# Attention output: query transposes two tiles ahead of the output products, output bias added by TensorE, norm statistics read from PSUM

## The reference

```python
q, k, v = split(x @ w_qkv)
q = softmax(q, axis=-1) / sqrt(64)
k = softmax(k, axis=1)
v = v / N
context = einsum('bnhd,bnhe->bhde', k, v)
out = einsum('bhde,bnhd->bhen', context, q) ... @ w_out + b_out
mu, var = mean(out, -1), mean((out - mu)**2, -1)
out = (out - mu) * rsqrt(var + 1e-5) * ln_scale
```

## Time and profile before

| | |
|---|---|
| Median of 3 runs | 2295.41 us (2293.19 to 2297.71) |
| The profiled execution | 2298.77 us, span 2297.0 us |
| Mean granted clock of PE | 0.968 |
| PE busy | 2076.6 us, 90% |
| DVE busy | 1340.3 us, 58% |
| ACT busy | 1045.3 us, 46% |
| Chain that ended last | PE 60%, DVE 14%, DMA 9%, issue 8% |

### The profile page before, as it was taken

One profiled execution on the slowest core, in us unless ns is written; L12 is line 12 of the kernel. 1 busy time (PEld: TensorE's weight loads), 2 busy tenths in 40 slices (PEclk: granted clock), 3 DMA queues, 4 the chain that ended last, 5 costly groups with the idle time before them and its releaser, 6 DMA issues.

```text
span 2297.0 us, 45572 instructions
## 1 busy us (share of the span) xinstructions
PE 2076.6 (90%) x13668; PEld 1497.5 (65%) x13669; DVE 1340.3 (58%) x2876; ACT 1045.3 (46%) x2324; POOL 628.5 (27%) x752
## 2 busy tenths in 40 slices
PE   4999788888888887899999999999599999879998
PEld 2544344344444445678888888888488888768886
DVE  2211588888888885655555555555722356664444
ACT  3731233333333332267776777777243232354443
POOL 2102487778788786120000000002200000000000
PEclk9999999999999998789999999999899999989999
DMA  9662367667676677454710440032700200210000
GB/s 211 218 162 88 97 190 192 186 187 190 183 191 187 188 191 288 184 210 165 288 41 28 159 169 18 18 133 84 274 24 10 82 20 19 99 49 10 10 10 18
DMA packets 200498, 291.09 MB, mean 127 GB/s; under 512 B 86076, under 2 KB 128202, under 8 KB 195949
## 3 DMA queue, kind: packets, MB, share of 16 engines
q1 hardware_dynamic: 153611, 159.22, 21.6%
q0 software_dynamic: 38208, 124.01, 18.5%
q10 hardware_dynamic: 8610, 6.94, 0.9%
HBM read 236.25 MB, written 53.85 MB: 126 GB/s over the span
## 4 chain that ended last, share of the span: by engine, by line
PE 60%; DVE 14%; DMA 9%; issue 8%; ACT 3%; SPq 2%; DVEq 2%; POOL 2%; POOLq 0%; ACTq 0%
PE psum L2547 14%; DMA big_b<-sender_table,wide 8%; PE psum L2685 6%; PE psum L2718 4%; PE psum L2537 4%; PE psum L2538 3%; PE psum L2539 3%; PE psum L2583 3%; DVE big_b L1720 3%; PE psum L2592 3%; DVE big_b L1721 3%; PE psum L2623 3%; PE psum L2613 2%; PE psum L2265 1%; POOL big_b L1025 1%
## 5 line engine op out<-in xcount | busy, mean ns | idle before, releaser
L1025 POOL DMA_INDIRECT big_b<-sender_table,wide x368 | 376.7, 1024 | 109.2 <-issue 87.2
L2396 PEld LDWEIGHTS psum<-big_b,wide 128*32 128x32 f32 x3680 | 170.0, 109 | 204.7 <-issue 138.3
L2366 PE MATMUL psum<-w_mlp,wide 64*128 64x512 f32 x744 | 212.4, 648 | 80.9 <-DVE big_b L1721 78.0
L2396 PE MATMUL psum<-big_b,wide 128*32 128x256 f32 (+2 forms) x3680 | 278.2, 390 | 4.4 <-POOL wide L1054 4.4
L2547 PEld LDWEIGHTS psum<-xn_T,big_b 128*128 128x128 f32 x2048 | 261.9, 191 | 21.2 <-issue 3.2
L2547 PE MATMUL psum<-xn_T,big_b 128*128 128x128 f32 x2048 | 265.0, 275 | 0.0
L1243 ACT ACTIVATE wide<-psum 128x384 f32<-128x384 f32 x45 | 22.1, 491 | 398.7 <-PE psum L2407 398.7
L1895 DVE TENSOR_TENSOR w_lo<-wide,w_hi 128x512 fp32r<-128x512 f32 x184 | 127.3, 692 | 117.9 <-ACT w_hi L1335 117.9
L2537 PE MATMUL psum<-w_hi,hid_hi 128*128 128x512 f32 x368 | 175.9, 478 | 9.4 <-DVE w_lo L1895 7.2
L1236 ACT ACTIVATE wide<-wide 128x290 bf16<-128x290 f32 x368 | 162.3, 527 | 47.5 <-PEq L2369 37.2
L1719 DVE TENSOR_TENSOR big_b<-psum,big_b 128x512 f32<-128x512 f32 x184 | 126.4, 687 | 91.6 <-DMA big_b<-sender_table,wide 77.2
(11 more groups left out here) (458 smaller groups left out, 3966.6 us busy)
## 6 DMA issues: line engine op xcount, KB each, us to landing
big_a<-in_L_ffn_W SPq DMA_DIRECT2D x12, 2048.0 KB, 13.9
big_b<-in_L_ffn_W SPq DMA_DIRECT2D x12, 2048.0 KB, 13.5
wide<-in_L_ffn_W SPq DMA_DIRECT2D x8, 2048.0 KB, 23.6
wide<-edge_hidden SPq DMA_DIRECT2D x186, 64.0 KB
edge_hidden<-wide SPq DMA_DIRECT2D x21, 512.0 KB, 2.8
tokens_sorted<-zeros SPq DMA_DIRECT2D x29, 256.0 KB, 3.3
adj_dram<-big_a SPq DMA_DIRECT2D x1, 6400.0 KB, 23.5
xn_T<-tokens_sorted POOLq DMA_DIRECT2D x25, 256.0 KB, 2.9
```

The costliest lines, as they stand in the source:

```text
L1025: nc.gpsimd.indirect_dma_start(out=sent[q][:, j, :], out_offset=None, in_=sender_table, in_offset=bass.IndirectOffsetOnAxis(ap=indices[j], ...
L2366: last = nc.tensor.matmul(tile_w[q % 2][:, j, :], h3_slot[q][halves[j], :], w_mlp4[halves[j], :], start=True, stop=True)
L2396: nc.tensor.matmul(msg_psum[k].rearrange("p (c u) -> p c u", u=MUL)[bands[g], cols, :], hot_y[q][:, j, y, :], p[:, of, :], start=False, st ...
```

## The change

The bank plan of the stage is one order, `att_order`: transposes of q tiles 0 and 1, then for each t the products of tile t and the transposes of tile t+2. PE follows it. ACT makes the leading part of tiles 0 and 1, and that of tile t+2 in round t, between the two square roots. DVE makes the rests of tiles 0 and 1, and that of tile t+2 in round t behind the first `moments`. PE opens each output bank with a matmul of a row of ones and the bias row (one row of contraction), and the bias add on DVE goes. `moments` reads the bank in PSUM, L2063's instruction reads it too and frees it. LAG becomes NT - Q_AHEAD = 8.

```diff
--- before.py
+++ after.py
@@ -582,7 +582,16 @@
         ring.plan([("kT", m, g) for m in range(C) for g in range(len(COLS))])
         ring.plan([("q", t) for t in range(NT)] + [("v", t) for t in range(NT)] + [("ek", t) for t in range(NT)])
         ring.plan([("ctxT",)] + [("m5", c) for c in range(C)])
-        ring.plan([("qT", t) for t in range(NT)] + [("att", t) for t in range(NT)])
+        Q_AHEAD = 2
+
+        def att_order():
+
+            yield from [("qT", t) for t in range(Q_AHEAD)]
+            for t in range(NT):
+                yield ("att", t)
+                if t + Q_AHEAD < NT:
+                    yield ("qT", t + Q_AHEAD)
+        ring.plan(list(att_order()))
 
         first_free = ring.at[("att", NT - 8)][0]
         result_banks, hidden_banks = ([(first_free + h + i) % 8 for i in range(4)] for h in (0, 4))
@@ -1477,14 +1486,18 @@
             for c in range(C):
                 full, _ = filled(act, ("m5", c))
                 nc.scalar.activation(m5_hi[:, c, :], full, ACT.Copy, scale=k_scale[:, c:c + 1]).then_inc(split_hi, 1)
-            for t in range(NT):
+            def queries_leading(t):
                 full, _ = filled(act, ("qT", t))
                 nc.scalar.activation(q_hi[:, :, tile_cols[t]], full.rearrange("p (c n) -> p c n", c=C), ACT.Copy).then_inc(split_hi, 1)
 
-            LAG = 4
+            for t in range(Q_AHEAD):
+                queries_leading(t)
+            LAG = NT - Q_AHEAD
             for t in range(NT + 2):
                 if t < NT:
                     root(t)
+                if t + Q_AHEAD < NT:
+                    queries_leading(t + Q_AHEAD)
                 if 1 <= t <= NT:
                     root(t - 1)
                 if t >= 2:
@@ -2044,24 +2057,28 @@
                 dve.wait_ge(split_hi, hi_no["m5", c])
                 nc.vector.scalar_tensor_tensor(m5_lo[:, c, :], full, k_scale[:, c:c + 1], m5_hi[:, c, :].bitcast(F32),
                                                ALU.mult, ALU.subtract).then_inc(free, 1)
-            for t in range(NT):
+            def queries_rest(t):
                 full, free = filled(dve, ("qT", t))
                 dve.wait_ge(split_hi, hi_no["qT", t])
                 nc.vector.tensor_tensor(q_lo[:, :, tile_cols[t]], full.rearrange("p (c n) -> p c n", c=C),
                                         q_hi[:, :, tile_cols[t]].bitcast(F32), ALU.subtract).then_inc(free, 1)
+
+            for t in range(Q_AHEAD):
+                queries_rest(t)
             dve.wait_ge(loads["b_out"], 48)
             last_numbers = {}
             for t in range(NT + 2):
                 if t < NT:
-                    full, free = filled(dve, ("att", t))
-                    nc.vector.tensor_tensor(att_rows[:, t, :], full, b_row["bk"][:, :], ALU.add).then_inc(free, 1)
-                    drained(dve, ("att", t))
-                    numbers[t] = moments(att_rows[:, t, :], t)
+                    full, _ = filled(dve, ("att", t))
+                    numbers[t] = moments(full, t)
+                    if t + Q_AHEAD < NT:
+                        queries_rest(t + Q_AHEAD)
                 if 1 <= t <= NT:
                     u = t - 1
                     inverse_roots(u, numbers[u])
-                    settle(nc.vector.scalar_tensor_tensor(att_rows[:, u, :], att_rows[:, u, :], meanvar[:, u, 0:1], b_row["bv"][:, :],
-                                                          ALU.subtract, ALU.mult))
+                    nc.vector.scalar_tensor_tensor(att_rows[:, u, :], bank(("att", u)), meanvar[:, u, 0:1], b_row["bv"][:, :],
+                                                   ALU.subtract, ALU.mult).then_inc(bank_free[ring.at["att", u][0]], 1)
+                    drained(dve, ("att", u))
                     settle(nc.vector.scalar_tensor_tensor(x_rows[:, u, :], att_rows[:, u, :], ln_root[:, u, 0:1], x_rows[:, u, :],
                                                           ALU.mult, ALU.add))
                     last_numbers[u] = moments(x_rows[:, u, :], u)
@@ -2668,14 +2685,22 @@
                 out_b, full = claim(pe, ("m5", c))
                 nc.tensor.matmul(out_b, kv_T[:, c, :], w_att[:, c, :], start=True, stop=True).then_inc(full, 1)
             pe.wait_ge(k_scale_ready, 1)
-            for t in range(NT):
-                pe.wait_ge(q_ready, t + 1)
-                transposes(("qT", t), chunks(q_rows[:, t, :]))
-            for c in range(C):
-                drained(pe, ("m5", c))
-            for t in range(NT):
+            pe.wait_ge(loads["b_out"], 48)
+            for kind, t in att_order():
+                if kind == "qT":
+                    pe.wait_ge(q_ready, t + 1)
+                    transposes(("qT", t), chunks(q_rows[:, t, :]))
+                    continue
+                if t == 0:
+                    for c in range(C):
+                        drained(pe, ("m5", c))
                 drained(pe, ("qT", t))
-                project("att", t, ((q_hi, m5_hi), (q_lo, m5_hi), (q_hi, m5_lo)))
+                out_b, full = claim(pe, ("att", t))
+                nc.tensor.matmul(out_b, ones_col[0:1, :].to_broadcast([1, P]), b_row["bk"][0:1, :], start=True, stop=False)
+                for c in range(C):
+                    for k, (lhs, rhs) in enumerate(((q_hi, m5_hi), (q_lo, m5_hi), (q_hi, m5_lo))):
+                        last = nc.tensor.matmul(out_b, lhs[:, c, tile_cols[t]], rhs[:, c, :], start=False, stop=(c == C - 1 and k == 2))
+                last.then_inc(full, 1)
 
             def hidden_columns(g, j):
 
```

## The result

The changed kernel takes 2306.4 us (2303.82 to 2314.41, six runs) against 2292.14 (2288.31 to 2297.71, six runs) beside it. The ratio is 1.0061, 95% interval 1.0042 to 1.0080: 14 us slower, between 10 and 18. Forecast was +9.0. The profiled execution took 2308.05 us, span 2306.3. One timed execution of the last experiment, e10, took 5179 us and is left out of its ratio.

A forecast was written before the change was run, and what follows sets the result against it. VectorE's program order, 4.83 us a round, was taken to bound the stage. +4.3 us until round 10 opens (front included) and +4.7 in the tail made +9.0 on a median of 2295.41: 2304.4 us, range 2298.5 to 2310.5 (8 in 10).

The forecast's parts named there:

- the wait for ACT: VectorE's rounds 1 to 7: the split waits out ScalarE's root and leading copy, 0.90 us each, +6.3 in all.
- the tail behind LAG = 8: Behind round 10: late ScalarE copies put four hidden groups there instead of two, +4.7 us (bounds +3.1 to +6.0).
- splits paid in the loop: VectorE's rounds 1 to 7: the split of q comes in at 0.61 us each, +4.3 in all.
- the front: Up to tile 1's products: splits taken out win nothing because VectorE waits for PE instead, tile 1 at 1982.2, +0.15 us.
- A short fall is swallowed by the round that PE is ahead: Argument against PE's clock falling in the loop: PE ends a tile's products a full round early, so short slowdowns cost nothing.
- -0.71, +0.61 and +0.90: Changes to VectorE's 4.83 us round: bias add gone, split of q in, new wait for ScalarE; 5.63 us.
- The rival in which the copy is no wait: ScalarE's copy lands before VectorE needs it: rounds 4.73 us, end up to 3.6 early, 2291.8; 4 in 100.
- Reads from PSUM: Statistics and row update read PSUM, not SBUF: taken at nothing, statistics allowed -0.05 to +0.1 us each.
- Round 10: Opens with VectorE's reciprocal after the output loop; forecast 4.3 us late, near 2029.5 instead of 2025.21.
- The rival that only half is paid: Tail's extra groups find room (2299.7), or the loop is paid less (about 2300); 14 in 100.
- The clock in the loop: Rival: PE idles 1.5 us a round, its clock falls and VectorE waits for PE, +21 us, 2325; 4 in 100.
- the bias part: VectorE's bias add goes for tiles 1 to 9, 0.71 us each, -6.4 in all; PE's bias product taken at 0.9.

The follow-up runs named there:

- e10: e5 plus e6's repeated transposes in PE's idle time of the front; stage 62.4 us, ratio 0.9992 against the kernel before.
- e1: The changed kernel with ScalarE's leading copy of q tile t+2 ahead of the square root of tile t; stage 70.1 us, ratio 1.0040.
- e6: The changed kernel with PE repeating the transposes of q tile 1 four times over while it waits for tile 0's split; stage 72.9 us, timed once.
- e5: e3 with ScalarE's leading copy of q made one tile further ahead (t+3); stage 65.5 us, ratio 0.9994.
- e2: The changed kernel with ScalarE's last copies in larger groups in rounds 8 to 11, not one a round; stage 71.6 us, ratio 1.0022.
- e4: The kernel before with only the bias product and statistics and row update from PSUM, LAG staying 4; stage 70.7 us, ratio 1.0040.
- e7: e4 with ScalarE's copies of the last transposes moved to rounds 9 and 10, between the roots; stage 59.5 us, ratio 0.9982.
- e8: The kernel before with bias / 8 added once to m5, statistics from PSUM, last copies moved to rounds 7 to 10; stage 57.8 us, ratio 0.9971.
- e3: The changed kernel with the edits of both e1 and e2; stage 66.4 us, ratio 1.0020.
- e9: The changed kernel without its bias part: VectorE adds the bias into SBUF rows again, order and LAG = 8 stay; stage 78.6 us, ratio 1.0073.

## Why the forecast held, point by point

The direction and the three mechanisms (the wait for ACT, the tail behind LAG = 8, splits paid in the loop) held; the front was mis-sized. That the forecast for the median, 2304.4 us, lies only 2 us from the measured 2306.4 is in part luck: with three more executions the kernel before has a median 3.3 us lower than the one that the forecast was added to. Taken as a difference, 14 us (12.2 in the stage) stands against +9.0, above the +7 to +12 of its own bounds.

**The front, forecast +0.15.** Wrong by 2.4 us, the worst term. Tile 1's statistics began at 1982.08, 14.2 us after the first rest of m5; forecast 11.8, before 11.6. By its parts: tile 0's products 4.44 where the way to tile 1 had 2.8 (1.6); two bias products 1.09 and 1.05 where 0.9 was taken (0.35); 0.24 until PE starts behind the split where 0.05 was taken (0.2); the transposes in between 0.53 for 0.44 (0.1); tile 1's products 3.00 where 2.95 was taken (0.05). The last 0.1 is a slip in the forecast's sum: its terms give 1982.29 for tile 1, not 1982.2. The first split starts 3.15 us after the first rest of m5, as before. At full clock the front would still be 1.0 worse than before (12.7 in e1, e6 and e10 against 11.6), so 1.5 of the miss is the clock's and 0.9 the prices of products and start. DVE's idle time ahead of tiles 0 and 1, named as a sign with some 3 and 1.4 us, was 5.29 and 1.88. The step that failed for the larger part was a sentence among the rivals: "A short fall is swallowed by the round that PE is ahead". That holds in the loop, and there it was seen: the clock read 0.73 between 2006 and 2011 (0.56 from 2008 to 2010), and rounds stayed at 5.62. In the front PE is not ahead of anything, and the fall was paid in full. I had counted PE's idle time there and asked nothing of its clock.

**The rounds.** -0.71, +0.61 and +0.90 gave 5.63; measured 5.62. The wait for ACT put the split 0.98 behind the start of L1764 (1993.95 to 1994.93) where 0.07 is the distance without one: 0.91 new, so the low part of 0.84 to 1.14 was right. e5 shows the wait is all of it (4.73 without), e1 and e5 that its cause is ACT's order. Rounds 8 and 9: 4.11 for 4.12. The rival in which the copy is no wait fell with this row.

**Reads from PSUM.** 0.70 at most for the statistics, against 0.69 to 0.70 from SBUF; the row update 0.75 from both. The Trainium skill's table (page "VectorE: DVE Perf Modes", section "The TRN2 errata"), which would add 0.065 us to each (an estimate from its cycles), is not borne out by these rows: the ten statistics from PSUM took 0.686 to 0.699, the row updates from PSUM 0.749 to 0.752.

**Round 10.** Forecast 4.3 late. Measured from the first rest of m5: 61.5 (2029.34 - 1967.86) against 54.8 (2025.21 - 1970.41), 6.7 late. The difference is the front's.

**The tail, forecast +4.7.** Measured 13.8 - 8.3 = 5.5. The mechanism is as told: two more groups behind round 10, held there by ACT's copies. e2 gives its length back, though by one group and the clock and not by two groups. 0.8 was missed in size: transposes began 1.56 behind round 10's start, not 1.4, and the slow pair took 1.08 and 3.62 where 1.12 and 3.14 stood in the earlier trace rows, with the next transposes in part slow too (0.79 for 0.60). A full-clock group costs 1.77 by the row that the forecast cites (14.18 / 8), not 1.73; that is 0.1 in all.

**The sum.** +9.0 forecast. +12.2 in the stage (front 2.6, rounds and their rest 4.1, tail 5.5), 14 (10 to 18) in the medians. The difference of 2 between the last two is inside the interval.

**The rival that only half is paid** would have needed copies ahead of round 10. One came there, tile 0's at 2026.07, and it releases only the transposes of tile 4; tile 1's, which the hidden groups need, came at 2030.18, behind round 10's opening at 2029.34. **The clock in the loop** fell once, a sign that the forecast had named as speaking against it, and cost nothing.

**What the forecast had not seen** was how the two parts stand to each other. I took the bias part as -6.4 with little against it. Alone it is a loss of 7.5 (e4), because of a wait of ACT's that has slack in the kernel before; with that wait moved it is a gain of 3.7 (e7). And its product is paid on PE ten times, where e8 pays five DVE instructions once.

**Open.** Whether the clock falls in the front because of the idle time ahead of it. It fell in the profiled executions of four of the six kernels with 1.55 to 1.60 us of idle there (changed, e2, e3, e5; not in e1 and e9). It fell in none of six without it: the two with that time filled (e6, e10), and before, e4, e7 and e8, where PE runs through. The DMA of the next weights, the rival named in e6, runs beside tile 0's products in all twelve, at a share of about 1.07, so it is not enough by itself. That points one way, with one profiled execution of each kernel, and what sets the four apart from the two is not shown.

## What to carry to other kernels

Before a step is moved into another engine's loop, write down both programs' orders around it: what counts is the instruction that stands ahead of the producer in its own queue and who releases that one. Moving work out of a front pays only as far as the next step had waited for that work; here eight splits moved into the loop brought tile 1 forward by 1.5 us and cost some 4 in the rounds (e10 against e7). Where a product adds a constant row and the other factor's rows sum to a known number, the constant can go into the small factor once.

## What had not been expected of the hardware

- The bias product is dear for what it computes. A plain f32 matmul with one row of contraction and 512 columns took 1.05 us in the chain, no less than one with 128 rows (0.89 from start to start, an estimate from the earlier trace rows), and with the twelve products at 3.00 a tile takes PE 4.05 us where it took 2.8: 1.25 more.
- In the front the granted clock fell after PE had gone back to work, not while it was idle. In the changed kernel and e3 it was some 2 us after: 1.00 through the idle time and the bias product, 0.53 in the middle of the products. In e2 and e5 it was within the bias product (1.63 and 1.53 us instead of 1.09). In the tail of the changed kernel it fell while PE still stood idle: 1.00 from 2026 to 2028, 0.68 from 2028 to 2030, with PE's next transposes at 2030.90.
